# Feed-forward on fp32 rows and fp32 gelu instead of hi and lo halves, and another order of the last tiles

## What is computed

```python
def _binarize(w):
    alpha = jax.lax.stop_gradient(jnp.mean(jnp.abs(w), axis=1, keepdims=True))
    bw = alpha * jnp.sign(w)
    return w + jax.lax.stop_gradient(bw - w)
...
D, H = (512, 2048)    # w1 (H, D), w2 (D, H)
```

## Time and profile before

| | us |
|---|---|
| median of 3 runs | 3588.18 |
| lowest and highest run | 3583.41 and 3593.11 |
| profiled execution, its own time | 3588.75 |
| span in its trace | 3587.4 |
| TensorE busy | 3224.2 (90% of the span) |
| VectorE busy | 2655.8 (74%) |
| ScalarE busy | 2388.7 (67%) |
| GpSimd busy | 1806.3 (50%) |

### The profile page before, as it was taken

One profiled execution on the slowest core, in us unless ns is written; L12 is line 12 of the kernel. 1 busy time (PEld: TensorE's weight loads), 2 busy tenths in 40 slices (PEclk: granted clock), 3 DMA queues, 4 the chain that ended last, 5 costly groups with the idle time before them and its releaser, 6 DMA issues. The chain is left out here.

```text
span 3587.4 us, 59841 instructions
## 1 busy us (share of the span) xinstructions
PE 3224.2 (90%) x20864; PEld 2259.3 (63%) x20864; DVE 2655.8 (74%) x4671; ACT 2388.7 (67%) x5339; POOL 1806.3 (50%) x1213
## 2 busy tenths in 40 slices
PE   5798989898898988988997998999999999999998
PEld 4566655665566655666554666666666666678787
DVE  2899999999999999999984776767766677622221
ACT  5777788777877788777863667666666667522221
POOL 2778887888878888888873000000000000055554
PEclk8899999999999999999998999999999999999999
DMA  5667666666666666676564041111211121020110
GB/s 166 162 175 196 188 167 157 184 175 188 168 161 182 190 171 160 175 196 180 159 166 155 6 124 59 46 46 65 71 46 46 51 78 66 18 76 24 36 35 24
DMA packets 286234, 425.03 MB, mean 118 GB/s; under 512 B 28689, under 2 KB 226065, under 8 KB 281330
## 3 DMA queue, kind: packets, MB, share of 16 engines
q1 hardware_dynamic: 278573, 411.44, 41.1%
q10 hardware_dynamic: 7365, 9.77, 0.9%
HBM read 320.12 MB, written 101.02 MB: 117 GB/s over the span
## 5 line engine op out<-in xcount | busy, mean ns | idle before, releaser
L810 POOL TENSOR_TENSOR a_hs<-a_rep,a_bmat 128x896 f32<-128x896 f32 x512 | 1061.0, 2094 | 291.0 <-PE a_yps L322 290.7
L442 ACT ACTIVATE a_states<-a_rep,a_a_neg 128x224 f32<-128x224 f32 x2048 | 793.5, 437 | 103.0 <-DVE a_hs L706 101.5
L699 DVE TENSOR_TENSOR_SCAN a_states<-a_states,a_hs 128x900 f32<-128x900 f32 x384 | 779.6, 2030 | 72.7 <-ACT a_states L442 57.9
L1403 DVE CUSTOM_DVE_ANT_0 b_sc<-sps,early_mask 112x375 f32<-112x375 f32 x1024 | 500.0, 545 | 154.1 <-PE sps L1146 153.9
L1162 PEld LDWEIGHTS b_tps<-ident,b_sc 112*125 112x125 f32 x3072 | 402.0, 191 | 286.4 <-issue 168.7
L1162 PE MATMUL b_tps<-ident,b_sc 112*125 112x112 f32 x3072 | 491.4, 289 | 77.3 <-DVE b_pT L1417 36.2
L1289 ACT ACTIVATE b_sc<-b_sc,b_nmax 112x750 f32<-112x750 f32 x512 | 467.4, 914 | 62.5 <-DVE b_nmax L1409 62.3
L1545 POOL TENSOR_SCALAR b_x_var<-mv 112x2 f32<-112x2 f32 x16 | 3.4, 213 | 889.2 <-DVE mv L1454 889.2
L344 PE MATMUL a_work<-early_scan_hT,w_in 128*128 128x224 f32 x2048 | 424.3, 363 | 8.9 <-issue 6.3
L706 DVE TENSOR_TENSOR a_hs<-a_states,a_cmat 128x896 f32<-128x896 f32 x384 | 419.2, 1092 | 13.2
L344 PEld LDWEIGHTS a_work<-early_scan_hT,w_in 128*128 128x128 f32 x2048 | 395.5, 196 | 49.1 <-issue 42.2
(11 more groups left out here) (194 smaller groups left out, 5011.4 us busy)
## 6 DMA issues: line engine op xcount, KB each, us to landing
a_rep<-du_scratch SPq DMA_DIRECT2D x512, 224.0 KB, 5.7
w_in<-W_in_dram SPq DMA_DIRECT2D x128, 512.0 KB, 4.4
du_scratch<-early_du SPq DMA_DIRECT2D x16, 1792.0 KB, 11.5
ctx<-ctxT_dram SPq DMA_DIRECT2D x48, 500.0 KB, 6.0
v_scratch<-kv_out SPq DMA_DIRECT2D x96, 250.0 KB
k_scratch<-kv_out SPq DMA_DIRECT2D x96, 250.0 KB, 4.5
b_keys<-k_scratch SPq DMA_DIRECT2D x8, 1500.0 KB, 8.6
b_v<-v_scratch SPq DMA_DIRECT2D x8, 1500.0 KB
```

Of the source, the lines that this page charges most:

```text
L442: e = act.activation(rows(states[:, g % DA, :])[:, q, 1:ROW], rep[tile % REPS][:, j, 0, :], ACT.Exp, scale=a_neg[:, g % SLOTS, q:q + 1])
L699: dve.tensor_tensor_scan(state if g % G4 else whole, state, whole, 0.0, ALU.mult, ALU.add).then_inc(S["scan"], 1)
L810: pool.tensor_tensor(hs[g % RING][:, :, 1:ROW], rep[tile % REPS][:, j, 1, :].unsqueeze(1).broadcast_to([P, Q, L]), bmat[b % 2][:], ALU.mul ...
L1403: dve.tensor_tensor_reduce(out=sc[block % 2][:, j, cols], in0=sps[0:TT, j, 0:HALF], in1=mask[:, block % 2, cols], scale=-1.0, scalar=3.0e3 ...
```

## The change

The halves go away. The rows `rowsT`/`hT` and the gelu output `gT` are single fp32 tiles, the signs are fp32 tiles, written by ScalarE in place over the raw weights, and each pair of matmuls on hi and lo becomes one matmul on fp32. ScalarE's gelu writes `gT` itself and now waits for the `second` that frees the buffer; both `split_g` are gone. VectorE copies the transposed rows from PSUM (`keep_h`, `keep_rows`) in place of ScalarE's copy and VectorE's subtraction. `prod` has four buffers in place of two. The last two pieces of the last step are computed tile by tile (`last_second`), the sums of its tiles 1 and 3 go to VectorE, and each tile is stored by a DMA of its own.

```diff
-        self.raw_1, self.s1 = mem.inside("raw_w1", [P, D // P, F], start), mem.inside("s1", [P, D // P, F], start, F32R)
+        self.s1 = mem.inside("s1", [P, D // P, F], start)
...
-            ("rowsT_hi", [P, KD, 4 * P], place["wq"], F32R), ("rowsT_lo", [P, KD, 4 * P], place["xt0"], F32R),
-            *((f"{name}_w2_{i}", [P, D], at, dtype) for name, dtype in (("raw", F32), ("sign", F32R))
+        for name, shape, at in (
+            ("x_0", [P, 4, D], place["keys0"]), ("x_1", [P, 4, D], place["hT"]),
+            ("x_2", [P, 4, D], place["hT"] + 4 * row), ("rows", [P, 4, D], place["v0"]),
+            ("rowsT", [P, KD, 4 * P], place["wq"]),
...
             def hidden(f):
                 pe.wait_ge(S["s1"], KD)
-                pe.wait_ge(S["rows_lo"], KD)
+                pe.wait_ge(S["rowsT"], KD)
                 pe.wait_ge(S["ttr"], GROUP * N_ALL)
                 for k in range(KD):
-                    for part in range(2):
-                        mm = pe.matmul(sps[:, f, 0:T], shared.s1[:, k, f * P:(f + 1) * P], rowsT[part][:, k, :],
-                                       start=(k == 0 and part == 0), stop=(k == KD - 1 and part == 1))
+                    mm = pe.matmul(sps[:, f, 0:T], shared.s1[:, k, f * P:(f + 1) * P], rowsT[:, k, :],
+                                   start=(k == 0), stop=(k == KD - 1))
                 mm.then_inc(S["f_ps"], 1)
...
-            def keep_rows(k):
-                act.wait_ge(S["unit"], unit_of["rows", k])
-                act.wait_ge(S["unit"], unit_of["q", B * GROUPS - 1, 0])
-                act.activation(rowsT[0][:, k, :], ups[:, bank_of["rows", k], :], ACT.Copy).then_inc(S["rows_hi"], 1)
...
-            def split_rows(k):
-                dve.wait_ge(S["rows_hi"], k + 1)
-                dve.wait_ge(S["unit"], unit_of["hT", B - 1, 1])
-                dve.wait_ge(S["xout0"], 16 * (B // 2))
-                dve.tensor_tensor(rowsT[1][:, k, :], ups[:, bank_of["rows", k], :], rowsT[0][:, k, :].bitcast(F32),
-                                  ALU.subtract).then_inc(S["rows_lo"], 1)
+            def keep_rows(k):
+                dve.wait_ge(S["unit"], unit_of["rows", k])
+                dve.wait_ge(S["unit"], unit_of["q", B * GROUPS - 1, 0])
+                dve.tensor_copy(rowsT[:, k, :], ups[:, bank_of["rows", k], :]).then_inc(S["rowsT"], 1)
...
-        hT = [[early["rowsT_hi"], early["rowsT_lo"]], [mem.sbuf(f"hT1_{n}", [P, KD, T], F32R) for n in ("hi", "lo")]]
-        g32 = [mem.sbuf(f"g32_{i}", [P, T]) for i in range(2)]
-        gT = [[mem.sbuf(f"gT{i}_{n}", [P, T], F32R) for n in ("hi", "lo")] for i in range(LAG + 1)]
-        prod = [mem.sbuf(f"prod{i}", [P, D]) for i in range(2)]
+        hT = [early["rowsT"], mem.sbuf("hT1", [P, KD, T])]
+        gT = [mem.sbuf(f"gT{i}", [P, T]) for i in range(LAG + 1)]
+        prod = [mem.sbuf(f"prod{i}", [P, D]) for i in range(TILES)]
...
                 for k in range(KD):
-                    for part in range(2):
-                        mm = pe.matmul(fps[:, n % 3, 0:T], s1[:, k, f * P:(f + 1) * P], hT[c % 2][part][:, k, :],
-                                       start=(k == 0 and part == 0), stop=(k == KD - 1 and part == 1))
+                    mm = pe.matmul(fps[:, n % 3, 0:T], s1[:, k, f * P:(f + 1) * P], hT[c % 2][:, k, :],
+                                   start=(k == 0), stop=(k == KD - 1))
...
             def second(n):
                 c, f = n // FT, n % FT
-                pe.wait_ge(S["g_lo"], n + 1)
+                pe.wait_ge(S["gelu"], n + 1)
                 if c == 0 and f and f % QUARTER == 0:
                     pe.wait_ge(S["sign"], f // QUARTER)
                 for i in range(TILES):
                     if f == 0 and c:
                         pe.wait_ge(S["prod"], TILES * (c - 1) + i + 1)
-                    for part in range(2):
-                        mm = pe.matmul(ops[:, i, :], gT[n % (LAG + 1)][part][:, i * P:(i + 1) * P], s2[f],
-                                       start=(f == 0 and part == 0), stop=(f == FT - 1 and part == 1))
+                    mm = pe.matmul(ops[:, i, :], gT[n % (LAG + 1)][:, i * P:(i + 1) * P], s2[f],
+                                   start=(f == 0), stop=(f == FT - 1))
                     if f == FT - 1:
                         mm.then_inc(S["o_tile"], 1)
                 if f < FT - 1:
                     mm.then_inc(S["o_ps"], 1)
+            def last_second():
+                pe.wait_ge(S["gelu"], ALL)
+                for i in range(TILES):
+                    for n in range(ALL - LAG, ALL):
+                        mm = pe.matmul(ops[:, i, :], gT[n % (LAG + 1)][:, i * P:(i + 1) * P], s2[n % FT],
+                                       start=False, stop=(n == ALL - 1))
+                    mm.then_inc(S["o_tile"], 1)
+
             for slot in slots:
                 if MADE <= slot < ALL:
                     hidden(slot)
-                if LAG <= slot < ALL + LAG:
+                if LAG <= slot < ALL:
                     second(slot - LAG)
+                if slot == ALL:
+                    last_second()
...
             def gelu(n):
                 f = n % FT
                 if n >= MADE:
                     act.wait_ge(S["f_ps"], n + 1 - MADE)
-                if n >= 2:
-                    act.wait_ge(S["g_lo"], n - 1)
-                act.activation(g32[n % 2][:], fps[:, n % 3, 0:T], ACT.Gelu, scale=alpha1[:, f:f + 1],
+                if n > LAG:
+                    after_second(act, n - LAG - 1)
+                act.activation(gT[n % (LAG + 1)][:], fps[:, n % 3, 0:T], ACT.Gelu, scale=alpha1[:, f:f + 1],
                                bias=b1[:, f:f + 1]).then_inc(S["gelu"], 1)
...
-            def split_h(c, k):
-                hi, lo = hT[c % 2]
-                dve.wait_ge(S["h_hi"], (c - 1) * KD + k + 1)
-                dve.tensor_tensor(lo[:, k, :], tps[:, 0:T], hi[:, k, :].bitcast(F32), ALU.subtract).then_inc(S["h_lo"], 1)
-
-            def split_g(n):
-                dve.wait_ge(S["gelu"], n + 1)
-                if n > LAG:
-                    after_second(dve, n - LAG - 1)
-                dve.tensor_copy(gT[n % (LAG + 1)][0][:], g32[n % 2][:]).then_inc(S["g_hi"], 1)
+            def keep_h(c, k):
+                dve.wait_ge(S["h_ps"], (c - 1) * KD + k + 1)
+                if c >= 2:
+                    dve.wait_ge(S["f_ps"], (c - 1) * FT - MADE)
+                dve.tensor_copy(hT[c % 2][:, k, :], tps[:, 0:T]).then_inc(S["hT"], 1)
             def scale_out(c):
                 for i in range(TILES):
                     m = c * TILES + i
                     dve.wait_ge(S["o_tile"], m + 1)
-                    if m >= 2:
-                        dve.wait_ge(S["sum"], m - 1)
-                    dve.tensor_tensor(prod[m % 2][:], ops[:, i, :], alpha2_row[:],
+                    if c:
+                        dve.wait_ge(S["sum"], TILES * (c - 1) + i + 1)
+                    dve.tensor_tensor(prod[i][:], ops[:, i, :], alpha2_row[:],
                                       ALU.mult).then_inc(S["prod"], 1)
+                    if c == STEPS - 1 and i % 2:
+                        dve.wait_ge(S["prod"], m + 1)
+                        dve.wait_ge(S["res"], c + 1)
+                        dve.tensor_tensor(xt[c % 3][:, i, :], xt[c % 3][:, i, :], prod[i][:],
+                                          ALU.add).then_inc(S["sum_dve"], 1)
...
-                hi, lo = gT[n % (LAG + 1)]
-                pool.wait_ge(S["g_hi"], n + 1)
-                pool.tensor_tensor(lo[:], g32[n % 2][:], hi[:].bitcast(F32), ALU.subtract).then_inc(S["g_lo"], 1)
...
-                for i in range(TILES):
+                for i in range(0, TILES, 2 if c == STEPS - 1 else 1):
                     m = c * TILES + i
                     pool.wait_ge(S["prod"], m + 1)
-                    pool.tensor_tensor(xt[c % 3][:, i, :], xt[c % 3][:, i, :], prod[m % 2][:],
+                    pool.tensor_tensor(xt[c % 3][:, i, :], xt[c % 3][:, i, :], prod[i][:],
...
+            def store_last():
+                c = STEPS - 1
+                for i in range(TILES):
+                    if i % 2:
+                        sp.wait_ge(S["sum_dve"], i // 2 + 1)
+                    else:
+                        sp.wait_ge(S["sum"], TILES * c + i // 2 + 1)
+                    sp.dma_start(out_tiles[:, TILES * c + i:TILES * c + i + 1, :],
+                                 xt[c % 3][:, i:i + 1, :]).then_inc(S[f"xout{c % 3}"], 16)
```

More of the change, by code:

```diff
@@ L104, in __init__ @@
         assert 4 * KEYS * KD >= 5 * row and KEYS // KC >= 6 and place["wo"] + KD * row >= place["hT"] + 8 * row
-        for name, shape, at, dtype in (
-            ("x_0", [P, 4, D], place["keys0"], F32), ("x_1", [P, 4, D], place["hT"], F32),
-            ("x_2", [P, 4, D], place["hT"] + 4 * row, F32), ("rows", [P, 4, D], place["v0"], F32),
-            ("rowsT_hi", [P, KD, 4 * P], place["wq"], F32R), ("rowsT_lo", [P, KD, 4 * P], place["xt0"], F32R),
```

(32 more changed lines are left out.)

37 lines of the change are left out of this document (12 added, 25 removed).

## The result

The changed kernel takes 3925.65 us (median of 4 runs, 3924.29 to 3930.78), the kernel before 3589.83 (median of 4): a ratio of 1.0936, with a 95% interval of 1.0922 to 1.0950. It is 335.8 us slower. The profiled execution took 3930.78 us, the longest of the four, with a span of 3929.5.

A forecast was written before the change was run, and what follows sets the result against it. TensorE's matmuls were taken to bound the feed-forward, the splitting lying beside them. Stage +341.3, seam +1.2, attention -1.0 and end -4.4 make +337.1 us on 3588.75: 3926 us, range 3914 to 3942 for 8 in 10.

The forecast's parts named there:

- The price of a matmul: Feed-forward: one fp32 matmul of 512 columns takes 0.859 us, in place of two fp32r matmuls of 0.464 together.
- the rival at 3543: Feed-forward: each fp32 matmul leaves one record of 0.4294 us, so the kernel gets faster, 3543 us; chance 0.03.
- The stage: Feed-forward, first second to last matmul: 771.3 us after, 430.0 before, so +341.3 us, with 1.8 for lost clock.
- The other side of the same sum: Feed-forward check: 349.2 us for matmuls, less 1.1 for the clock and 7.3 for product waits, gives 340.8.
- The seam: Between attention and feed-forward: the first second starts later, +1.2 us (0.7 to 2.5).
- the two candidates for the barrier: Seam: TensorE or SyncE's statistics store reaches the barrier last; first gelu at 3148.5 to 3150.3, taken as 3149.0.
- Attention: Attention: ScalarE loses four row copies of 0.58 us; between 0 and 2.3 us gained, taken as -1.0.
- The end: Last matmul to end of span: 4.4 us instead of 8.8, so -4.4 us (-3.9 to -5.0).
- The sum: Whole kernel: 341.3 + 1.2 - 1.0 - 4.4 = +337.1 us on the profiled 3588.75, forecast 3926 us.
- The signs: Feed-forward trace: two records per matmul, hidden 3.43 us, slot 6.87, step 111.6, clock 1.00, no product waits.
- Wide spacing of records: Feed-forward: fp32 records lie 0.4425 us apart instead of 0.4294, +23 us, 3949 us; chance 0.04.
- One record: Feed-forward: one record of 0.4294 us per fp32 matmul instead of two, stage -38.3 us, 3543 us; chance 0.03.

The follow-up runs named there:

- the third experiment: The kernel before with only the first product in fp32, the second still in hi and lo halves: 3759.00 us, ratio 1.0457 to the kernel before.
- the second experiment: The changed kernel with two product buffers, the old order of the last pieces and one 1 MB store: 3929.90 us, ratio 1.0938 to the kernel before.
- first experiment: The kernel before, halves kept, with four product buffers and the last pieces computed, summed and stored tile by tile: 3583.13 us, ratio 0.9976 to the kernel before.

## Why the prediction was right, step by step

- **The price of a matmul** (0.859 us, two records) was read from L374, another place of the program with other tiles (L403 gave only the wider spacing of a rival). In the feed-forward it is 0.858. This is the step on which the result hung, and the count of records was its decisive part: whoever takes the 0.43 us between two records of an fp32 run for a matmul forecasts a faster kernel (the rival at 3543). The page after excludes that: 20864 records, although 896 instructions have gone.
- **The stage**, +341.3 us predicted, is +341.3 in the profile (771.3). The sum holds 1.8 us for a slow start; measured, the first eight records took 5.23 us from their start to the next piece instead of 3.43 to 3.44, 1.8 lost. In the fp32 kernel without the new end and in the one with 256 columns the same start, after 2.04 us of idle time instead of 2.33, lost 0.1. So this term lay between 0.1 and 1.8; whether the length of the idle time or the execution decides is not shown.
- **The other side of the same sum** (349.2 for the matmuls, less 7.3 for the product waits) is borne out: the third experiment needs both to come to its 163.3, within 1 or 2 us.
- **The seam**, +1.2: it is +1.19. First gelu 1.5 us after TensorE's last early product, within the 1.0 to 2.8 that the two candidates for the barrier gave. In the kernel of the second experiment TensorE started at 3138.76 and its gelu 11.67 later instead of 11.95.
- **Attention**, -1.0. Between two marks on TensorE, a wait of 0.25 us for an exponential ahead of the four row copies and the start of the last output projection behind them, there are 30.01 us in this profile (3104.91 to 3134.92) and 30.18 before (3100.36 to 3130.54); that is a gain of 0.2. But in the four other kernels with the copies on VectorE it is 28.51 or 28.52, and in the two others with ScalarE's copies 29.77 and 29.76: 1.25 gained. The term had its size right, and the profiled execution of the changed kernel shows less of it. In this stretch its granted clock fell twice (0.53 from 3108 to 3112, 0.67 from 3124 to 3128), in the second experiment's profile once (0.50 from 3124 to 3128).
- **The end**, -4.4: it is -5.2. A store of 256 KB landed 2.0 us after its issue, not in the 2.4 to 3.4 that I took from a load; the last store follows its sum directly. By the second experiment 4.0 of the 5.2 are the new end and 1.2 the slower tiles of fp32, a split that the prediction didn't make.
- **The sum** of 3926 stands against a median of 3925.65. For the profiled execution the terms give 341.3 + 1.2 - 0.2 - 5.2 = 337.1; its span has grown by 342.1, and the 5 us between are those that came before 3141.85 and that other executions don't show. The exact agreement is therefore partly luck: single executions of one kernel differ by as much as the edges are worth, and in the profile the 0.8 us by which the end was undersized cancels the 0.8 by which attention was oversized.
- **The signs.** A step takes 111.7 us (twelve slots of 6.87 and four of 7.31), 111.6 forecast; TensorE waits for no product. The granted clock is 1.00 in the middle of the stage, as forecast for the denser load, but not in the first microseconds, for which the sum held its 1.8 (the last section has the rows).
- **The rivals.** Wide spacing of records (3949): no, the switch between kinds every eight records costs nothing (3.43 us from each piece to the next). One record: no.
- The Trainium skill's four passes for true FP32 ("FP8 and Floating Point Precision", TensorE Precision Notes) agree with the fp32 rows: an fp32 matmul of 512 columns takes 0.859 us, four times the 0.216 of a bf16 one. That each of its two records is two passes fits their 0.429 us, and no run shows it more directly. Its gap of columns / 2.4 + 2.5 ns ("TensorE: Matmul & The Clock Gate", Back-to-back issue gap), 215.8 ns at 512 columns, is what bf16 does here (0.216 us), and what fp32r doesn't (0.234 and 0.229). The measurement decides: the sum by the pages was 375 us, the one by the rows 349, and the rows were right.

## What to carry to other kernels

An fp32 matmul of 512 columns costs 0.859 us here, four times a bf16 one, and shows in a trace as two records of 0.43: count records against instructions before a price is read from a spacing. Where one operand is exact in a short format (signs), two halves of the other in fp32r (0.464 us) or bf16 (0.432 us) are about half the price of fp32. Their splitting lies beside TensorE in the middle of such a stage, and shows only at its edges: the first `second` came 2.63 us after the start of its gelu with the halves and 0.84 without, and the tile-by-tile end waited 0.87 us for the last lo half. Removing work that TensorE doesn't wait for gains nothing in a stage where TensorE is busy 99% of the time.

## What the runs showed of the hardware that was not expected

- fp32r matmuls of 512 columns are spaced at 0.234 us (first product) and 0.229 (second), bf16 ones at 0.216, with the same instructions around them and a granted clock of 1.00 in both. What holds fp32r back by 13 to 18 ns was not tried. The weight loads differ too, 0.188 us each with fp32r and 0.098 with bf16; against their length as the whole reason stands that fp32 records of 256 columns ran at 0.216 over loads of 0.190.
- After a short idle time the clock can fall or not, and the length alone doesn't tell. After 2.33 us of idle time at the seam of the changed kernel the granted clock fell, only after the first matmuls had begun; after 2.04 us in two other kernels it did not, and after 1.97 us at L374 before, 1.8 us were lost again. The stretches of the changed kernel, clock in the column before the DMA share:

```profile
3154.00:3156.00 2.00, 1.36 (x3) 0.68 (x4) 0.00 (x0) 1.92 (x3) 2.00 (x2) 1.00 0.54 67
3156.00:3158.00 2.00, 2.00 (x4) 0.94 (x3) 0.00 (x0) 0.00 (x0) 2.00 (x3) 0.51 1.04 397
3158.00:3160.00 2.00, 2.00 (x4) 0.73 (x4) 0.00 (x0) 0.91 (x1) 0.74 (x1) 0.63 1.00 363
3160.00:3162.00 2.00, 2.00 (x6) 0.82 (x5) 0.00 (x0) 1.00 (x1) 0.00 (x0) 1.00 1.00 378
```

- VectorE's sum of 128 x 512 fp32 took 0.69 us alone and 1.26 us beside a GpSimd sum of the same kind (first experiment); GpSimd's took 1.26 to 1.29 in both. VectorE's product, which reads PSUM, kept its 0.69 us beside GpSimd's sums (before, at 3579.52).
